# First stage of a two-layer kernel: eight convolution slots, rates staged whole, loads issued by GpSimd, a zero fill moved

## The reference, cut to what matters

```python
x  = hidden_states                     # (8, 512, 128) f32
xn = layernorm(x)
# layer 0, branch s: a chunked recurrence
q = l2norm(silu(short_conv(xn @ Wq.T, cq)))        # k the same way; v without l2norm
lr = softplus(xn @ Wlr.T + 1e-3)                   # two rates per head and token
for chunk in range(32):                            # 16 tokens a chunk, 16 heads, 8 batches
    o, W_in, W_out = step(W_in, W_out, q[chunk], k[chunk], v[chunk], lr[chunk])
s = (norm(o) * ln_g + ln_b) * (xn @ Wg.T) @ Wo.T
# layer 0, branch g: top 2 of 8 experts for each token
g = silu(moe(xn))
x = x + s * g
# layer 1: layernorm, a selective scan (conv, delta, B, C) as s, a capacity-limited top-2
# mixture of experts as g, and again x + s * g
```

## Time and profile before

| | |
|---|---|
| three executions | 1386.91 us median (1386.6 to 1388.56) |
| profiled execution | 1388.35 us; its span, first to last instruction, 1386.6 us |
| instructions | 15822 |
| DVE / PE / ACT / POOL busy | 1236.4 (89%) / 986.0 (71%) / 697.6 (50%) / 686.1 us (49%) |
| memory read / written | 108.06 MB / 39.04 MB |

### The profile page before, as it was taken

How to read it: one execution, slowest core, us unless ns; L and a number is a source line. 1 busy time by engine, 2 the same in 40 slices (tenths; PEclk the granted TensorE clock), 3 DMA queues, 4 the chain that set the end, 5 groups by cost and what they waited for, 6 DMA issues and landing times. The chain is left out here.

```text
span 1386.6 us, 15822 instructions
## 1 busy us (share of the span) xinstructions
PE 986.0 (71%) x3622; PEld 576.3 (42%) x3623; DVE 1236.4 (89%) x2319; ACT 697.6 (50%) x1319; POOL 686.1 (49%) x623
## 2 busy tenths in 40 slices
PE   3775233877777877777743587648898898888874
PEld 2142232555555555555533552224444343444331
DVE  6779895999999999999999978999897788979899
ACT  4563112455555455554432327537666667666751
POOL 5004772232223222222301006789798789788895
PEclk9877556899899899999975678979999999999998
DMA  9579211000000000000052305447434435444346
GB/s 305 153 205 312 69 46 32 20 22 19 19 22 21 19 17 19 22 23 18 6 154 91 91 1 178 130 120 200 178 139 151 152 127 173 154 157 163 109 171 186
DMA packets 106867, 145.49 MB, mean 105 GB/s; under 512 B 26443, under 2 KB 82520, under 8 KB 101952
## 3 DMA queue, kind: packets, MB, share of 16 engines
q1 hardware_dynamic: 91232, 118.70, 27.6%
q0 software_dynamic: 9920, 21.12, 4.3%
q10 hardware_dynamic: 5664, 5.11, 1.2%
HBM read 108.06 MB, written 39.04 MB: 106 GB/s over the span
## 5 line engine op out<-in xcount | busy, mean ns | idle before, releaser
L2041 DVE TENSOR_TENSOR ps<-ps,cv 128x512 f32<-128x512 f32 x256 | 163.2, 683 | 21.5 <-ACT ps L1570 20.6
L1106 PE MATMUL ps<-Q,ident 128*128 128x512 f32 x256 | 137.8, 630 | 35.5 <-DVE Q L2059 22.4
L759 POOL DMA_INDIRECT y_tok<-xnT,meta x72 | 75.4, 1048 | 175.2 <-ACT xnT L1307 160.7
L815 POOL TENSOR_TENSOR Q<-LR,xn 128x512 f32<-128x512 f32 x96 | 122.6, 1277 | 28.8 <-PE ps L1106 14.4
L736 POOL DMA_INDIRECT slots_x<-xn,sl_put x64 | 76.8, 1200 | 113.7 <-issue 113.4
L945 PE MATMUL ps<-wd_a,xn 128*128 x576 | 96.8, 319 | 36.7 <-ACT xn L1301 36.7
L945 PEld LDWEIGHTS ps<-wd_a,xn 128*128 128x128 f32 x576 | 81.9, 219 | 49.5 <-issue 48.0
L529 POOL TENSOR_TENSOR x<-x 128x512 f32<-128x512 f32 x27 | 31.8, 1176 | 141.7 <-DVE x L1845 141.7
L928 PE MATMUL ps<-wg_a,xnT 128*128 x144 | 91.1, 720 | 12.7 <-issue 11.6
L1319 ACT ACTIVATE x<-x 128x128 f32<-128x128 f32 (+1 forms) x127 | 31.9, 277 | 132.1 <-DVE x L1902 59.0
L963 PE MATMUL ps<-x,ident 128*128 128x128 f32 x256 | 43.1, 323 | 69.9 <-DVE x L529 36.8
(11 more groups left out here) (343 smaller groups left out, 2807.2 us busy)
## 6 DMA issues: line engine op xcount, KB each, us to landing
cv<-bc_scr SPq DMA_DIRECT2D x64, 512.0 KB, 4.0
xn<-bc_scr SPq DMA_DIRECT2D x24, 1024.0 KB, 4.9
O<-bc_scr SPq DMA_DIRECT2D x8, 1024.0 KB, 5.7
slots_x<-O POOLq DMA_DIRECT2D x28, 260.0 KB, 5.6
qkv_scr<-cv SPq DMA_DIRECT2D x24, 256.0 KB, 4.7
xnT<-slots_x SPq DMA_DIRECT2D x72, 64.0 KB, 1.8
x<-in_x SPq DMA_DIRECT2D x8, 512.0 KB, 5.8
y_tok<-O SPq DMA_DIRECT2D x1, 4096.0 KB, 22.4
```

What stands on the lines that cost most here:

```text
L759: pool.indirect_dma_start(out=y_tok, out_offset=bass.IndirectOffsetOnAxis(ap=meta_bits[:, n, 0:1], axis=0), in_=yg[:, k, :], in_offset=Non ...
L815: pool.tensor_tensor(yc_g0[:, n % 4, :], st_g0[:, n % 2, :], cn, ALU.mult).then_inc(yc_ready, 1)
L1106: pe.matmul(ps[:, 4, :], ident[:], yc_g0[:, n % 4, :], start=(n == 0), stop=(n == NS - 1)).then_inc(y0_used, 1)
L2041: tt(dBu(g), ps[:, 2 + g, :], b_rows[:, n % 4, :], ALU.mult).then_inc((inject0, b_used)[g], 1)
```

## The change

Five things, all in the first stage or at its end.

1. The convolutions go through eight slots, `ring`, which lies in `wg_a` (the gate weights, loaded later) in the place of the four of `cv`. `tap(cu)` waits for the store of `cu - 8`. SP loads `wg_a` after all stores have landed. At the start ACT takes `tap(0)`, `tap(1)` and `tap(2)` earlier among its normalising, and the Silu table load comes after `tap(2)`, followed by `silu(0)` and `silu(1)` together.
2. The rates are copied into `lr_rows`, 32 partitions of `gateT`, whole: no copy waits for a store. PE alternates two banks. SP stores them with one DMA of 512 KB after the store of convolution 17.
3. The six `heads_load` and the load of `LZ` are issued by POOL, between its buffer fills and its scatters.
4. On DVE the wait for `LZ` and the addition to it (line 1737) stand before `dispatch(0)`; on ACT the three passes over the rates (lines 1282 to 1284) follow the routing exponential.
5. The zero fill of `y_tok1` is no longer a 4 MB write from SBUF by SP. POOL issues it as two DMAs from memory to memory after its 64 scatters, reading 4096 rows of 512 B (pitch 520 B) of the already zeroed `slots_x1` each. The wait before step 0 is gone; POOL waits for the fill before layer 1's scatter.

```diff
-                if cu >= 4:
-                    act.wait_ge(stored[cu % 4], 16 * (cu // 4))
-                act.activation(cv[:, cu % 4, :], ps[:, 2 + cu % 4, :], ACT.Copy, scale=...)
+                since(act, stored[cu % 8], 16 * (cu // 8))
+                act.activation(ring[:, cu % 8, :], ps[:, 2 + cu % 4, :], ACT.Copy, scale=...)
...
-                if b >= 2:
-                    act.wait_ge(lr_stored[b % 2], 16 * (b // 2))
-                act.activation(LR[0:2 * H, b % 2, :], ps[0:2 * H, 7, :], ACT.Copy)
+                act.activation(lr_rows[:, b * L:(b + 1) * L], ps[0:2 * H, 6 + b % 2, :], ACT.Copy)
...
             for cu, (w, b) in enumerate(CONVS):
                 sp.wait_ge(silu_done, cu + 1)
+                sp.dma_start(qkv_scr[w, b], ring[:, cu % 8, :]).then_inc(stored[cu % 8], 16)
                 if cu == 2 * B + 1:
+                    sp.wait_ge(lr_copied, B)
+                    sp.dma_start(lr_scr.rearrange("b r t -> r b t"), lr_rows.rearrange("r (b t) -> r b t", b=B))
+            for u in range(8):
+                sp.wait_ge(stored[u], 16 * NCU // 8)
             sp.dma_start(wg_a[:], d["wg_a"]).then_inc(we_loaded, 16)
...
-            sp.wait_ge(pad_ready, 1)
-            sp.dma_start(y_tok1.rearrange("(i p) c -> p i c", p=P), bc(pad[:, 0, 0:D], 1, 2 * NT))
...
+            heads_load(0, 1, K, k_in)          # on POOL
+            heads_load(1, 1, K, k_in)
+            heads_load(0, 0, Q, q_in)
+            heads_load(1, 0, Q, q_in)
+            pool.wait_ge(lr_stored, 16)
+            pool.dma_start(LZ, lr_scr.rearrange("b (h j) t -> (b h) j t", h=H)).then_inc(lr_landed, 16)
+            heads_load(0, 2, V, v_in)
+            heads_load(1, 2, V, v_in)
             pool.wait_ge(zeroed, ZEROED)
             pool.wait_ge(slots_ready, 1)
...
                     pool.indirect_dma_start(out=slots_x, ...)      # the 64 scatters
+            for j in range(2):
+                pool.dma_start(y_tok1[j * T:(j + 1) * T, :], slots_x1[0:T, 0:D]).then_inc(y1_zeroed, 16)
...
-            act.wait_ge(y1_zeroed, 16)
             step(0, False, start=True)
...
             dve.wait_ge(consts_ready, 6)
+            dve.wait_ge(lr_landed, 16)
+            dve.tensor_scalar_add(LZ, LZ, 1e-3).then_inc(lr_in, 1)
             dispatch(0)
```

More of the change, by code:

```diff
@@ L201, in build @@
         logit_bank, rank_bank = (0, 1), (1, 2)
+        ring = wg_a[:].rearrange("p (u t) -> p u t", t=L)
+        lr_rows = gateT[0:2 * H, :]
         sq_k, sq_q = (a[:].rearrange("p (e t) -> p e t", e=HD) for a in (wd_a, wu_a))
@@ L335, in build @@
         lr_copied = sem("lr_copied")
-        stored = [sem(f"stored{i}") for i in range(4)]
-        lr_stored = [sem(f"lr_stored{k}") for k in range(2)]
+        stored = [sem(f"stored{i}") for i in range(8)]
+        lr_stored = sem("lr_stored")
         k_in, q_in, v_in, lr_landed = (sem(n) for n in ("k_in", "q_in", "v_in", "lr_landed"))
@@ L542, in _ @@
                 sp.dma_start(dst, d[src]).then_inc(w_loaded, 16)
[L544 to L550, removed]
             sp.wait_ge(xn_ready, NT // 2)
@@ L555, in _ @@
                 sp.wait_ge(silu_done, cu + 1)
[L556 to L562, removed]
+                sp.dma_start(qkv_scr[w, b], ring[:, cu % 8, :]).then_inc(stored[cu % 8], 16)
                 if cu == 2 * B + 1:
[L564 to L567, removed]
+                    sp.wait_ge(lr_copied, B)
+                    sp.dma_start(lr_scr.rearrange("b r t -> r b t"), lr_rows.rearrange("r (b t) -> r b t", b=B)).then_inc(lr_stored, 16)
+            for u in range(8):
+                sp.wait_ge(stored[u], 16 * NCU // 8)
             sp.dma_start(wg_a[:], d["wg_a"]).then_inc(we_loaded, 16)
@@ L723, in _, with heads_load @@
                                pad).then_inc(zeroed, 16)
+            def heads_load(half, w, dst, done):
+                turn = 2 * (1, 0, 2).index(w) + half
+                for u in range(4):
+                    pool.wait_ge(stored[4 * (turn % 2) + u], 16 * (turn // 2 + 1))
+                pool.dma_start(dst[half * 64:(half + 1) * 64, :, :],
+                               qkv_scr[w, 4 * half:4 * half + 4].rearrange("b (h e) t -> (b h) e t", h=H)).then_inc(done, 16)
+            heads_load(0, 1, K, k_in)
[6 more added lines that the diff above has]
+            heads_load(1, 2, V, v_in)
             pool.wait_ge(zeroed, ZEROED)
@@ L899, in _ @@
                 project(B + b)
-                since(pe, lr_copied, b)
-                pe.matmul(ps[0:2 * H, 7, :], wlr[:], xnT[:, b * L:(b + 1) * L], start=True, stop=True).then_inc(lr_ps, 1)
+                since(pe, lr_copied, b - 1)
+                pe.matmul(ps[0:2 * H, 6 + b % 2, :], wlr[:], xnT[:, b * L:(b + 1) * L], start=True, stop=True).then_inc(lr_ps, 1)
             for b in range(B):
@@ L1219, in tap @@
                 act.wait_ge(proj_ps, cu + 1)
-                if cu >= 4:
-                    act.wait_ge(stored[cu % 4], 16 * (cu // 4))
-                act.activation(cv[:, cu % 4, :], ps[:, 2 + cu % 4, :], ACT.Copy, scale=taps[:, CONVS[cu][0], 3:4]).then_inc(tap_first, 1)
+                since(act, stored[cu % 8], 16 * (cu // 8))
+                act.activation(ring[:, cu % 8, :], ps[:, 2 + cu % 4, :], ACT.Copy, scale=taps[:, CONVS[cu][0], 3:4]).then_inc(tap_first, 1)
             def silu(cu):
                 act.wait_ge(conv_done, cu + 1)
-                act.activation(cv[:, cu % 4, :], cv[:, cu % 4, :], ACT.Silu).then_inc(silu_done, 1)
+                act.activation(ring[:, cu % 8, :], ring[:, cu % 8, :], ACT.Silu).then_inc(silu_done, 1)
             def lr_copy(b):
                 act.wait_ge(lr_ps, b + 1)
-                if b >= 2:
-                    act.wait_ge(lr_stored[b % 2], 16 * (b // 2))
-                act.activation(LR[0:2 * H, b % 2, :], ps[0:2 * H, 7, :], ACT.Copy).then_inc(lr_copied, 1)
+                act.activation(lr_rows[:, b * L:(b + 1) * L], ps[0:2 * H, 6 + b % 2, :], ACT.Copy).then_inc(lr_copied, 1)
             def square(t, sq, e):
@@ L1244, in _ @@
             xnT_copy(1)
-            norm_rows(5)
             act.wait_ge(taps_ready, 1)
             tap(0)
-            norm_rows(7)
+            norm_rows(5)
             xnT_copy(2)
             tap(1)
+            norm_rows(7)
+            tap(2)
+            xnT_copy(3)
             act.preload_act_table(ACT.Silu)
-            for cu in range(2, NCU):
+            for cu in range(3, NCU):
                 if cu + 1 < G4:
                     xnT_copy(cu + 1)
-                silu(cu - 2)
+                if cu > 3:
+                    silu(cu - 2)
+                else:
+                    silu(0)
+                    silu(1)
                 tap(cu)
@@ L1268, in _ @@
             act.activation(route[0].lg, route[0].lg, ACT.Exp).then_inc(probs_ready, 1)
+            act.wait_ge(lr_in, 1)
+            o.link(act.activation(LR[:], LZ, ACT.Abs))
+            o.link(act.activation(LR[:], LR[:], ACT.Exp, scale=-1.0))
+            act.activation(LR[:], LR[:], ACT.Ln, bias=1.0).then_inc(lr_log, 1)
             act.preload_act_table(ACT.Sqrt)
@@ L1273, in _ @@
                 square(Q, sq_q, 2 * k)
+            act.wait_ge(lr_stored, 16)
             for b in range(B):
@@ L1722, in _ @@
                 for sh in (1, 2, 3):
-                    i = dve.scalar_tensor_tensor(cv[:, s, sh:L], ps[:, 2 + s, 0:L - sh], taps[:, w, 3 - sh:4 - sh],
-                                                 cv[:, s, sh:L], ALU.mult, ALU.add)
+                    i = dve.scalar_tensor_tensor(ring[:, cu % 8, sh:L], ps[:, 2 + s, 0:L - sh], taps[:, w, 3 - sh:4 - sh],
+                                                 ring[:, cu % 8, sh:L], ALU.mult, ALU.add)
                     if sh < 3:
```

11 lines of the change are left out of this document (2 added, 9 removed).

## The result

The changed kernel takes 1373.59 us in the median of four executions (1371.6 to 1373.82), the kernel before 1387.74 beside it; the ratio is 0.9892, with a 95% interval of 0.9876 to 0.9907. That is 14.2 us less by the medians and 15 by the ratio (13 to 17).

The account below looks back on a forecast made before the run. Bound: one chain of convolutions, dispatch, slot numbers, 64 scatters and first tile. It ends 16 us earlier, less 2 us for the fill: 14 us, so 1373 us, between 1368 and 1379 (1366 to 1388 with most rivals).

Parts of the forecast that it names:

- The chain: First stage up to step 3: everything after hangs on convolutions, dispatch, slot numbers, 64 scatters, first tile; its end 16 us earlier.
- Convolutions: Convolution loop: starts at 21.0, 53.8 us at DVE's pace plus 2.0 us of stall, ends at 76.8.
- PE's cover: Convolution loop: PE may run three convolutions ahead, 6.7 us, hiding one low clock spell; nothing charged, 5 us kept for range.
- Rates in front: Before dispatch: DVE waits 0 to 5.3 us for the rates, 1.5 us taken, plus 0.7 us for the addition.
- Dispatch: Between convolutions and scatters: starts at 79.0 instead of 95.52 and keeps its 24.0 us.
- Scatters: POOL's 64 scatters: the first is released sooner, 0.6 us more; the last comes at 201 to 203.
- The wait before step 0: DVE's wait of 5.05 us before step 0: its removal is worth nothing, since the wait in step 3 grows.
- The fill: Zero fill behind the scatters: POOL's issue 3 to 6 us each, within cover; the first tile's load delayed by 2 us.
- C: After the scatters: POOL's fill takes 8 to 14 us each, outlasting its cover but not the gain; 1375 to 1387, chance 0.09.
- D: After the scatters: the fill's issue goes by rows, 17.4 us each, making the kernel slower at 1392; chance 0.10.
- B: First stage: the loop gives half back, the gain is 14 less 5 to 8 us; 1378 to 1383, chance 0.16.
- E: Step 3 doesn't hang on the tile, so the 5 us of step 0 count too; about 1366 or less, chance 0.05.

Follow-up runs that it names:

- fill_sp: The changed kernel with the zero fill given back to SP from the zero tile and ACT waiting for it before step 0; 1369.73 us, ratio 0.9859.
- fill_only: The kernel before with only the zero fill issued by POOL behind the scatters and no wait before step 0; ratio 1.0044.
- psum_norm: The changed kernel with DVE reading the reciprocal norms from PSUM in the two multiplications of K and Q; 1367.67 us, ratio 0.9847.
- both_moves: The changed kernel with the two fill DMAs moved to POOL's turn of step 12 and the norms read from PSUM; 1363.44 us, ratio 0.9821.
- fill_mid: The changed kernel with its two fill DMAs moved from behind the 64 scatters to POOL's turn of step 12; 1370.84 us, ratio 0.9870.
- rates_halves: The changed kernel with the rates staged by halves as before, eight slots kept; ratio 1.0049.

## Why the prediction was right, point by point

- **The chain** (convolutions, dispatch, scatters, first tile) was right, and it is what carried the result. fill_sp, fill_only and psum_norm each move a stall that is on it or off it, and the time follows the chain alone.
- **Convolutions.** Worked out: end at 76.8, dispatch at 79.0. Measured: 77.4 and 78.6. The 2.0 us of remaining stall were 4.6 less the first 1.8, so 2.8. The first starts at 20.84 (21.0), and from 29.55 to 74.1 sixty instructions run without a gap, 2.23 us for three.
- **PE's cover** was tested harder than I had charged for and held: from 60 to 78 us PE was busy all the time at the low level, the very state that I feared, at 3.4 us a convolution (3.5 to 4 worked out), and its lead was used up only at the last convolution, by a stall of 0.93 us. Charged nothing; it cost about 1 us. One of those stretches (columns as above), and ACT's last tap, which waits for PE:

```profile
65.00:70.00 5.00, 5.00 (x15) 3.45 (x16) 4.86 (x8) 4.78 (x8) 1.09 (x2) 0.50 1.11 285
...
74.34 0.69 ACT L1228 ACTIVATE wg_a<-ps,taps 128x512 f32<-128x512 f32 x1 [1.77 <-PE ps L889]
```

- **Rates in front.** A wait of 1.5 us charged, 0.59 measured: the store landed in 4.6, the load in 9.0 us. The range of 0 to 5.3 was real: 4.4 in both_moves.
- **Dispatch** kept its 24.0 us less 0.7: ACT's table load now lies beside the addition. I had missed that.
- **Scatters.** 0.6 expected, 1.4 measured. The first row is 4.41 for 5.00. Most of the rest, 0.7, is a copy of POOL between two scatters (line 734), 0.94 us long before and 0.23 now; the 62 other scatters are only 0.2 shorter together. The last scatter ends at 199.7, ahead of the 201 to 203 that the prediction gave.
- **The wait before step 0**: worth nothing, as said. DVE waited 25.4 us in step 3 for the 21 or 22 expected, the difference being mostly the late tile.
- **The fill.** The step that was mis-sized, in both halves. POOL's issue was put at 3 to 6 us for 4096 rows and measured 1.65 and 1.59, so the price by rows, on which rivals C and D stood, is out: 32 times the rows cost three times the 0.55 us. The Trainium skill, "DMA: Bandwidth & Descriptors", section on the anatomy of a GpSimd-issued DMA, has many descriptors emitted before the incremental cost shows; it was the better guide, and the trace agrees with it in part: 32 times the rows add 1.1 us, not nothing. The two fills cost POOL's chain nothing, for `q_product(4)` still waits 9.8 us for DVE behind them. The delay of the first tile was put at 2 us and is 4.7: the quick issue puts the first 2 MB ahead of the tile's load (199.72 against 201.05) and the second 1.2 us behind it, and the fills land in 11.8 and 15.2 us. The tile comes more than 6 us after its issue, which was one of the signs of being wrong that the prediction named (over 4 us); that the order of the two issues is what matters is argued, not tested. Low price and high delay belong together, which I had noted and not followed.
- **The sum**: 16 - 2 = 14 forecast. On the same terms 19.0 - 4.7 = 14.3 measured. The chain came out 3 us better than worked out, and the tile 2.7 worse: the total is closer than its terms, and that is luck.
- **Rivals.** B (loop gives back half), C and D (POOL's issue) did not occur. E, that stalls add up, is excluded by fill_sp.

## What to carry to other kernels

Before costing a stall, find the last wait behind it: here one engine's idle time in step 3 absorbed every saving that was not on the way to the last scatter, and the part of the change that removed a visible wait of 5 us made the kernel slower. A bulk transfer issued in the same breath as the last small transfer of a chain delays the next load on that chain; put it some steps later, where loads are ahead of their use. When two buffers both stall a loop, cure both or expect little: curing one left from a quarter or a third of the gain down to less than nothing.

## What the runs showed of the hardware that was not expected

- POOL's issue of an indirect DMA is held up to the end of a DVE tensor_tensor with both inputs in SBUF (4.41 and 4.75 us instead of 1.05 and less), and takes 1.05 us beside it when one input is in PSUM. The DVE instruction takes 4.42 us either way. The Trainium skill, "SBUF — State Buffer", in its list of the operations that take the shared pair of ports, does name tensor_tensor, which the prediction said it leaves out: with both inputs in SBUF it contends with GpSimd's reads, and the page infers that it spares descriptor writing. Both fit the runs, if the reading of the slot numbers is what is held up: the scatters are held, and the plain DMAs of fill_mid are not (3.23 us for two). No run tests that reading by itself.
- A POOL-issued DMA of 4096 rows of 512 B takes 1.6 us to issue, one of 128 rows 0.55.
- Two transfers of 2 MB from memory to memory beside it put the landing of a 64 KB load at up to 11.5 us, from a median of 1.9.
- PE held the low level for 18 us and for over 20 while busy all the time (60 to 78 in the changed kernel, from 80 to past 100 in rates_halves).
